# Quantised feed-forward of a gated two-layer block: the clip and the rescaling of the activations move from VectorE to ScalarE and GpSimd, in a pipeline over half tiles

## What is computed

```python
def _quantize_mx(x, ebits, mfrac, emax_elem, max_norm):        # blocks of 32 along the last axis
    amax = jnp.max(jnp.abs(xb), axis=-1, keepdims=True)
    sexp = jnp.floor(jnp.log2(jnp.where(amax == 0, 1.0, amax))) - emax_elem
    scale = jnp.exp2(jnp.clip(sexp, -127.0, 127.0))
    return _quantize_elem(xb / scale, ebits, mfrac, max_norm) * scale
def _q_act(x): return _quantize_mx(x, 2, 3.0, 2.0, 7.5)
def _mx_linear(x, w): return jnp.einsum('bsh,oh->bso', _q_act(x), _q_w(w))
gate = _mx_linear(x, w_gate)          # 512 -> 2048
up = _mx_linear(x, w_up)              # 512 -> 2048
inter = jax.nn.silu(gate) * up
return _mx_linear(inter, w_down)      # 2048 -> 512
```

## Time and profile before

| what | before |
|---|---|
| median of 3 runs | 1871.81 us |
| the profiled execution: its own time | 1870.53 us |
| its span | 1868.7 us |
| mean granted TensorE clock | 0.894 of full speed |
| busy: PE, DVE, ACT, POOL | 1484.8, 1112.7, 980.8, 635.6 us |
| stage B, from the scale of its layer norm to its last moments | 401.6 to 721.1 us |

### The profile page before, as it was taken

The page is one execution under the profiler, slowest core; times in us unless marked ns, Lnnn a source line. Parts: engine busy times, 40 slices in busy tenths (PEclk is TensorE's granted clock), DMA queues, the critical chain, the costliest instruction groups (busy, mean ns, idle before and its releaser), DMA issues. The chain is left out here.

```text
span 1868.7 us, 31243 instructions
## 1 busy us (share of the span) xinstructions
PE 1484.8 (79%) x10376; PEld 777.9 (42%) x10395; DVE 1112.7 (60%) x1785; ACT 980.8 (52%) x1503; POOL 635.6 (34%) x557
## 2 busy tenths in 40 slices
PE   6666666677776775999999711899999999999994
PEld 2444455543333332444444310444444444444442
DVE  3999999788888896888886472205415140541000
ACT  4999999733232233777777440344444444444442
POOL 3000000010000000788888535435445444544432
PEclk9778777788898897999999765999999999999998
DMA  9311100000000000000000256315335151531113
GB/s 336 135 46 46 46 1 1 29 1 1 0 0 0 0 0 1 3 2 3 2 3 3 88 190 249 117 35 163 111 86 168 26 165 34 163 95 34 30 28 102
DMA packets 49246, 118.69 MB, mean 64 GB/s; under 512 B 5536, under 2 KB 5792, under 8 KB 48576
## 3 DMA queue, kind: packets, MB, share of 16 engines
q1 hardware_dynamic: 34832, 88.53, 14.0%
q0 software_dynamic: 8176, 18.65, 5.1%
q10 hardware_dynamic: 6144, 10.28, 1.8%
HBM read 84.21 MB, written 37.43 MB: 65 GB/s over the span
## 5 line engine op out<-in xcount | busy, mean ns | idle before, releaser
L1622 PE MATMUL PS<-R 128*128 (+1 forms) x1872 | 432.7, 381 | 8.3 <-issue 7.2
L1776 DVE TENSOR_SCALAR R<-wring 128x1024 f16<-128x1024 f32 x56 | 61.5, 1108 | 382.6 <-PE PS L1645 349.2
L425 ACT ACTIVATE R<-R 128x512 bf16<-128x512 f32 x448 | 278.9, 715 | 9.4 <-PE PS L445 3.9
L1622 PEld LDWEIGHTS PS<-R 128*128 128x128 f16 x1872 | 179.5, 98 | 217.6 <-issue 19.7
L445 PE MATMUL PS<-R,ident_b 128*128 128x256 bf16 (+1 forms) x1056 | 168.6, 321 | 83.1 <-ACT R L425 79.1
L1645 PE MATMUL PS<-R 128*128 (+1 forms) x936 | 214.8, 379 | 1.2 <-ACT R L1732 1.2
L1812 POOL TENSOR_TENSOR R<-R 128x512 f32<-128x512 f32 x78 | 113.3, 1453 | 292.0 <-ACT R L1720 181.0
L871 PE MATMUL PS<-R 128*128 128x512 bf16 x495 | 141.9, 436 | 78.6 <-DVE R L807 60.4
L1036 DVE TENSOR_REDUCE R<-PS 128x1 f32<-128x512 f32 x256 | 166.6, 686 | 45.2 <-PE PS L1218 42.6
L1014 POOL TENSOR_TENSOR R<-R 128x512 f32<-128x512 f32 x128 | 166.6, 1302 | 27.8 <-ACT R L1141 12.2
L1141 ACT ACTIVATE R<-PS 128x512 f32<-128x512 f32 x256 | 144.4, 598 | 41.3 <-PE PS L1232 40.8
(11 more groups left out here) (262 smaller groups left out, 2522.3 us busy)
## 6 DMA issues: line engine op xcount, KB each, us to landing
wring<-in_L_ffn_w_kernel_dram SPq DMA_DIRECT2D x48, 512.0 KB, 5.3
slot_rows<-R SPq DMA_DIRECT2D x1, 10023.0 KB, 40.3
R<-slot_rows ACTq DMA_DIRECT2D x39, 257.0 KB, 2.7
R<-in_L_ffn_w_kernel_dram SPq DMA_DIRECT2D x16, 512.0 KB, 5.6
wring<-in_L_ffn_wo_kernel_dram SPq DMA_DIRECT2D x16, 512.0 KB, 4.5
R<-in_L_ffn_wo_kernel_dram SPq DMA_DIRECT2D x16, 512.0 KB, 4.7
X<-in_x_dram SPq DMA_DIRECT2D x4, 1024.0 KB, 9.0
R<-in_L_ffn_w_up_dram SPq DMA_DIRECT2D x4, 1024.0 KB, 10.3
```

The source lines that it names most:

```text
L425: nc.scalar.activation(marks[:, j * S:(j + 1) * S], SIM[:, tile * S:(tile + 1) * S], ACT.Sign, bias=cfloat[:, tile:tile + 1], scale=-1.0). ...
L1622: mm = nc.tensor.matmul(bank[2 * half + g], ZT[n][:, (4 * pz + k) * P:(4 * pz + k + 1) * P], weights(place, at), start=(i % 12 == 0), stop ...
```

## The change

The z quantisation and the inter quantisation are each cut in three. VectorE keeps the first part: block maxima, exponent bits, scale, reciprocal, and the rounding product, which now writes its fp8 result to a buffer of its own (bzq, biq). ScalarE copies the fp8 values to bf16 (z_widen, inter_widen). GpSimd clips them in place between CAP and -CAP and multiplies them by the scale (z_final; inter_final, in two pieces of 512). The exponent bits are taken by a tensor_tensor with a constant tile bexp and the scale by a scalar_tensor_tensor with a constant tile b16, where both were tensor_scalar.

The halves are numbered u = 0 to 31, with two buffers each of bin_, biq, bic, bib, bit2 and two PSUM banks (4 and 7) for the transposed half, and four of each scale. TensorE transposes half u-2 and multiplies half u-3 by the down weights behind gate and up of half u+1; before, both belonged to the half just made. VectorE adds tile i to X at half u = 2i+5. All loops of B are written out.

```diff
+CAP = 7.5 / 64
-        bin_ = R1[:, 11008:12032]
-        bib = R1[:, 12032:12544].bitcast(BF16)
-        bit2 = R1[:, 12544:13056].bitcast(BF16)
+        bin_ = [R1[:, 11008:12032], R1[:, 0:1024]]
+        biq = [R1[:, 1024 + 256 * n:1280 + 256 * n].bitcast(F8) for n in range(2)]
+        bic = [R1[:, 2048 + 512 * n:2560 + 512 * n].bitcast(BF16) for n in range(2)]
+        bib = [R1[:, 12032:12544].bitcast(BF16), R1[:, 3072:3584].bitcast(BF16)]
+        bit2 = [R1[:, 12544:13056].bitcast(BF16), R1[:, 3584:4096].bitcast(BF16)]
...
+            nc.gpsimd.memset(bexp, EXPONENT).then_inc(const_b, 1)
+            nc.gpsimd.memset(b16, 16.0).then_inc(const_b, 1)
...
-        def quantize_act(v, src, n, dst, base, done):
-
-
-            nb = n // BLK
-            am, pw, sc, ri = bam[:, 0:nb], bpw[:, 0:nb], bsc[:, 0:nb], bri[:, 0:nb]
...
-            nc.vector.tensor_scalar(bq[:, 0:n], bf8[:, 0:n], 7.5 / 64, -7.5 / 64, ALU.min, ALU.max).then_inc(q_step, 1)
-            v.wait_ge(q_step, base + 6)
-            nc.vector.tensor_tensor(blocks(dst), blocks(bq[:, 0:n]), spread(sc, nb), ALU.mult).then_inc(done, 1)
+        def scales(v, src, am, pw, sc, ri, n, step, base):
+            nc.vector.tensor_reduce(am, blocks(src), AX, ALU.max, apply_absolute_value=True).then_inc(step, 1)
+            v.wait_ge(step, base + 1)
+            nc.vector.tensor_tensor(pw.bitcast(I32), am.bitcast(I32), bexp[:, 0:n], ALU.bitwise_and).then_inc(step, 1)
+            v.wait_ge(step, base + 2)
+            nc.vector.scalar_tensor_tensor(out=sc, in0=pw, scalar=TINY, in1=b16[:, 0:n], op0=ALU.max,
+                                           op1=ALU.mult).then_inc(step, 1)
+            v.wait_ge(step, base + 3)
+            nc.vector.reciprocal(ri, sc).then_inc(step, 1)
+            v.wait_ge(step, base + 4)
...
+            def z_scale(j):
+                v.wait_ge(z_ready, j + 1)
+                if j > 3:
+                    v.wait_ge(zb_ready, j - 3)
+                scales(v, bz, zam, zpw, zsc[j % 4], zri, D // BLK, z_step, j * 4)
+                if j:
+                    v.wait_ge(z_wide, j)
+                nc.vector.tensor_tensor(blocks(bzq), blocks(bz), spread(zri, D // BLK), ALU.mult,
+                                        saturate=False).then_inc(z_cut, 1)
...
+            def inter_scale(u):
+                v.wait_ge(inter_ready, 2 * u + 2)
+                if u > 3:
+                    v.wait_ge(ib_ready, 2 * u - 6)
+                scales(v, bin_[u % 2], bam, bpw, bsc[u % 4], bri, 1024 // BLK, i_step, u * 4)
+                if u > 1:
+                    v.wait_ge(i_wide, u - 1)
+                nc.vector.tensor_tensor(blocks(biq[u % 2]), blocks(bin_[u % 2]), spread(bri, 1024 // BLK), ALU.mult,
+                                        saturate=False).then_inc(i_cut, 1)
...
+            z_scale(0)
+            z_scale(1)
+            for u in range(2 * NT):
+                for n in range(2):
+                    product(u, n)
+                if u % 2 and u > 4:
+                    residual((u - 5) // 2)
+                inter_scale(u)
+                if u % 2 == 0 and u // 2 + 2 < NT:
+                    z_scale(u // 2 + 2)
+                if u % 2 and u > 4:
+                    moments((u - 5) // 2)
+            residual(NT - 2)
+            moments(NT - 2)
             dve_ln_var(v, 2, 0)
-            chain(NT - 1, 1, (NT - 1) * 18 + 12)
-            finish(NT - 1)
+            residual(NT - 1)
+            moments(NT - 1)
+
+        def pool_b(pool):
+            def z_final(j):
+                pool.wait_ge(z_wide, j + 1)
+                if j:
+                    pool.wait_ge(zt_ps, j)
+                nc.gpsimd.tensor_scalar(bzc, bzc, CAP, -CAP, ALU.min, ALU.max).then_inc(z_capped, 1)
+                pool.wait_ge(z_capped, j + 1)
+                pool.wait_ge(z_cut, j + 1)
+                nc.gpsimd.tensor_tensor(blocks(bzb), blocks(bzc), spread(zsc[j % 4], D // BLK), ALU.mult).then_inc(zb_ready, 1)
+
+            def inter_final(u):
+                pool.wait_ge(i_wide, u + 1)
+                pool.wait_ge(i_cut, u + 1)
+                if u > 1:
+                    pool.wait_ge(it_ps, u - 1)
+                for n in range(2):
+                    c = slice(512 * n, 512 * n + 512)
+                    nc.gpsimd.tensor_scalar(bic[u % 2][:, c], bic[u % 2][:, c], CAP, -CAP, ALU.min, ALU.max).then_inc(i_capped, 1)
+                    pool.wait_ge(i_capped, 2 * u + n + 1)
+                    nc.gpsimd.tensor_tensor(blocks(bib[u % 2][:, c]), blocks(bic[u % 2][:, c]),
+                                            spread(bsc[u % 4][:, 16 * n:16 * n + 16], 16), ALU.mult).then_inc(ib_ready, 1)
+
+            z_final(0)
+            z_final(1)
+            for u in range(2 * NT):
+                inter_final(u)
+                if u % 2 == 0 and u // 2 + 2 < NT:
+                    z_final(u // 2 + 2)
...
+            for u in range(2 * NT + 3):
+                if u + 1 < 2 * NT:
+                    gate_up(u + 1, 0)
+                    gate_up(u + 1, 1)
+                if u % 2 == 0 and u // 2 + 1 < NT:
+                    zturn(u // 2 + 1)
+                if u == 2 * NT + 1:
+                    pe_projection(pe)
+                if 0 <= u - 2 < 2 * NT:
+                    turn(u - 2)
+                if 0 <= u - 3 < 2 * NT:
+                    down(u - 3)
...
+            def z_widen(j):
+                act.wait_ge(z_cut, j + 1)
+                if j:
+                    act.wait_ge(zb_ready, j)
+                nc.scalar.copy(bzc, bzq).then_inc(z_wide, 1)
...
+            def inter_widen(u):
+                act.wait_ge(i_cut, u + 1)
+                if u > 1:
+                    act.wait_ge(ib_ready, 2 * u - 2)
+                nc.scalar.copy(bic[u % 2], biq[u % 2]).then_inc(i_wide, 1)
...
+            for u in range(2 * NT + 2):
+                if 0 <= u - 1 < 2 * NT:
+                    inter_widen(u - 1)
+                if u == 2 * NT:
+                    act_projection(act)
+                if u + 1 < 2 * NT:
+                    silu(u + 1, 0)
+                if u % 2 and u // 2 + 2 < NT:
+                    z_widen(u // 2 + 2)
+                    if u // 2 + 3 < NT:
+                        norm(u // 2 + 3)
+                if u + 1 < 2 * NT:
+                    silu(u + 1, 1)
+                if 0 <= u - 2 < 2 * NT:
+                    icopy(u - 2)
+                if u % 2 == 0 and u // 2 + 1 < NT:
+                    zcopy(u // 2 + 1)
```

More of the change, by code:

```diff
@@ new lines, in dve_b, with product, residual @@
+        def dve_b(v):
+            def z_scale(j):
[7 more added lines that the diff above has]
+                                        saturate=False).then_inc(z_cut, 1)
+            def product(u, n):
+                v.wait_ge(silu_sb, 2 * u + n + 1)
+                v.wait_ge(gu_ps, 4 * u + 2 * n + 2)
+                nc.vector.tensor_tensor(bin_[u % 2][:, n * 512:(n + 1) * 512], bsg[:, n * 512:(n + 1) * 512],
+                                        bank[2 + n], ALU.mult).then_inc(inter_ready, 1)
+            def inter_scale(u):
[7 more added lines that the diff above has]
+                                        saturate=False).then_inc(i_cut, 1)
+            def residual(i):
+                v.wait_ge(down_ps, 2 * i + 2)
+                xt = X[:, i * D:(i + 1) * D]
@@ L837, in dve_b @@
-            for i in range(2):
-                prep(i, i * 6)
-                v.wait_ge(zb_ready, i + 1)
-            body(0, first=True)
-            with v.Fori(1, NT - 2) as i:
-                body(i)
-            body(NT - 2, last=True)
-            chain(NT - 1, 0, (NT - 1) * 18 + 6)
-            v.wait_ge(ib_ready, 2 * NT - 1)
-            finish(NT - 2)
-            dve_ln_var(v, 2, 0)
-            chain(NT - 1, 1, (NT - 1) * 18 + 12)
-            finish(NT - 1)
+            v.wait_ge(const_b, 2)
@@ L859, in zturn, with gate_up @@
                 mm.then_inc(zt_ps, 1)
[L861 to L867 removed]
+            def gate_up(u, n):
+                if u % 2 == 0 and n == 0:
+                    pe.wait_ge(zt_sb, u // 2 + 1)
+                if u:
+                    pe.wait_ge(inter_ready, 2 * u + n - 1)
                 for m in range(2):
@@ L880, in turn, with down @@
                 for c in range(8):
-                    mm = nc.tensor.transpose(bank[4].bitcast(BF16)[:, c * P:(c + 1) * P],
-                                             bib[:, c * P:(c + 1) * P], ident_b[:])
+                    mm = nc.tensor.transpose(bank[7 if u % 2 else 4].bitcast(BF16)[:, c * P:(c + 1) * P],
+                                             bib[u % 2][:, c * P:(c + 1) * P], ident_b[:])
                 mm.then_inc(it_ps, 1)
-            def down(i, half):
-                pe.wait_ge(it_sb, 2 * i + half + 1)
-                if half == 0 and beyond(i, 0):
-                    pe.wait_ge(x2_done, i)
+            def down(u):
+                pe.wait_ge(it_sb, u + 1)
+                if u % 2 == 0 and u:
```

(25 more changed lines are left out.)

175 lines of the change are left out of this document (47 added, 128 removed).

## The result

The changed kernel takes **1793.16 us** (median of 4 runs, 1790.0 to 1794.91) against 1872.28 us for the kernel before (4 runs, 1865.91 to 1873.47): ratio 0.9582, 95% interval 0.9556 to 0.9608. That is 79 us less, where the prediction had 49. The profiled execution took 1792.18 us, with a span of 1790.3.

What follows compares the result with a forecast made beforehand. VectorE's instructions were taken to bound stage B. Start 26, middle 219.5 (14 tiles of 16.0 less 4.5) and end 26 made 271.5 against 319.5 us, 48 less: 1870.5 - 48 = 1822.5, say 1823 us; range 1792 to 1856.

Steps and rivals of the forecast that it cites:

- the prediction's own case: Whole kernel: 1808 to 1836 us, around 1823, with VectorE setting stage B's pace and some port waits; chance 0.50.
- rival 1: Stage B: the shared ports cost nothing, 13.6 us per tile, 1789 us in all; chance 0.12.
- 16.0 us per tile: Middle of stage B: VectorE's own work 13.1, port waits 2.4 and 0.5 carried over from before.
- 13.1 us: VectorE in stage B: its remaining instructions per tile, gaps included, after clips and scale products leave.
- 2.4 us: Stage B: VectorE's waits per tile for ports shared with GpSimd, if blocked instructions end early; otherwise 4.0.
- the walk: One stage B tile followed, GpSimd starting 1.25 us after VectorE's rounding product, each taking free ports when asked.
- The 0.5 that before had over its own sum: VectorE's tile in stage B: 19.15 us measured against 18.6 summed, put to loop branches and cross-engine waits, kept as 0.5.
- priced at nothing by itself: VectorE's exponent and scale as two-input instructions of 16 or 32 elements: still 0.17 to 0.18 us, no added cost.
- since the rewrite: VectorE's exponent and scale: counted among instructions contending with GpSimd because they now have two SBUF inputs, six of 0.18 us.
- Rival 2: Stage B: the port exclusion costs more, 17 to 18 us per tile, 1837 to 1851 us in all; chance 0.20.
- Rival 3: Stage B: GpSimd becomes the bound and is slower than before, 20.4 us per tile, 1885 us; chance 0.10.
- Rival 4: Stage B: the pipeline gives nothing, TensorE is held and VectorE waits for gate and up, about 1868 us; chance 0.08.

Runs made afterwards that it cites:

- e2: The changed kernel with GpSimd's clips and scale products in stage B replaced by memsets of the same size: 1774.37 us, 12.27 us per tile.
- e6: The changed kernel with ScalarE casting the even half ahead of its two copies, so GpSimd starts earlier: 1796.21 us.
- e7: The changed kernel with GpSimd's clip and product of an inter half each as one instruction of 1024 instead of two of 512: 1800.31 us.
- e4: The changed kernel with every GpSimd clip in stage B done twice: 1810.65 us.
- e3: The changed kernel's order, buffers and depth, but clip and scale product back on VectorE, no cast, GpSimd idle: 1861.62 us, 0.9937 of the kernel before.
- e1: The changed kernel with exponent and scale taken by one-input tensor_scalar instructions again, as before the change: 1791.37 us.
- e9: The changed kernel without pipeline depth, TensorE transposing the half just made, work still on ScalarE and GpSimd: 1998.49 us, 1.0678 of the kernel before.

## Why the prediction was right, and where it was off

The direction and the mechanism held: VectorE stays the pace (96% busy), TensorE fits under it, GpSimd and ScalarE don't bind, and the stages around B don't move. The size was 30 us short: 1793 lies 15 us under the 1808 to 1836 of the prediction's own case and 1 us inside the stated range, which reached so low only for the upper half of rival 1, so that the range holds it is in part luck. The middle was to take 219.5 us and took 189.2, 30.4 less. Start and end, predicted at 26 each, took 24.1 and 23.6, and the 4.3 us that they were better cancel by chance against the 4.3 that the rest of the program was longer.

The middle rests on the term "16.0 us per tile" (measured: 13.51 on average, 13.61 steady). Its three parts:

- **"13.1 us" of VectorE's own work was 12.2** (e2). The durations were right: 1.22, 0.35 and 1.22 for what stands alone, and 0.19 for exponent and scale, for which the 0.18 of the earlier trace rows belongs to the one-input form. The gaps were not. The prediction put 0.04 us between all neighbours, but that holds only where one waits for the other. Independent ones overlap: the rounding product from 501.08 for 1.57 ends at 502.65, and z's maxima start at 502.57; the two products and the addition likewise (504.59 + 1.28, next at 505.78).
- **"2.4 us" for the ports was 1.38** in the steady tile, 1.24 by e2. The rule was right, the walk's phases were not. It let GpSimd begin 1.25 us after each rounding product. For the even half it was 2.24 (502.65 to 504.89), because the cast (503.75 to 504.81) stood behind ScalarE's copies of the transposed half and of z (502.36 and 503.27), and so z's rounding product met nothing. GpSimd was also faster than priced, 0.61 and 1.05 unblocked instead of 0.76 and 1.16, with 0.09 between them instead of 0.15, and the odd rounding product met an opening. e6 shows that the phase alone is worth some 0.4 us per steady tile, and e7 and e4 that longer GpSimd instructions cost what the exclusion says.
- **"The 0.5 that before had over its own sum"** did not come back. The trace of the kernel before has it where a tile's loop turns: ahead of the tile's first product VectorE stands idle behind its own last instruction, 14 times and 7.9 us, 0.56 per tile. For TensorE it waits 2.5 us at the products in the whole stage, and 2.8 at the additions. e3 and the change, with the loops written out, have no such pause. Waits of the kernel before, 430 to 698 us:

```profile
DVE R L807 <- DVE R L789: 7.9, 14, 0.6
```

Together 0.9 + 1.0 + 0.5 = 2.4 us per tile, 33.5 us in 14 tiles. Against them stands that the prediction took 4.5 us off for what tiles 1 and 14 lack, where the middle is only 1.4 shorter than 14 steady tiles, its uneven first tiles included: 33.5 - 3.1 = 30.4.

The other steps: exponent and scale "priced at nothing by itself" is right (e1). But it is not "since the rewrite" that they meet GpSimd, as the one-input form waits as well. The cast of 1.05 took 1.052. TensorE's wait "below 40" is 27.1, the clock "above 0.88" is 0.98. The written-out loops cost nothing, as said, and with them the pause above is gone.

The rivals. Rival 1, that the ports cost nothing, gave 1789 us, nearer the result than my own case, and is nevertheless refuted: e2 shows 19 us of port waits. Its number came close because its base of 13.6 per tile was too high by as much as the ports cost: 0.9 of own work and 0.5 of loops, against 1.4. Rival 2 (17 to 18 per tile) did not occur: blocked instructions end early, 1.08 after the release, and in the steady tile only three meet anything. Rival 3 needed a pair of 2.8 us and the pair is 1.66; neither the repeated operand nor 16 bits cost anything. Rival 4 did not occur here, but e3 and e9 show how near it lies: the pipeline without the shift to the other engines is worth only 0.6% [0.4%, 0.8%], and the shift without the pipeline loses 6.8% [6.5%, 7.1%]. With the pipeline there, the shift brings the other 68 us.

## What to carry to other kernels

Work may go from a saturated VectorE to GpSimd even though GpSimd is slower at it, if the consumer runs far enough behind that GpSimd's latency is hidden; make that depth first, since without it the same shift turned 4% of gain into 7% of loss. Price the shared ports by laying both engines' instructions side by side in time, with the start of GpSimd's work taken from everything queued on the engine that feeds it, and keep GpSimd's pieces short. When VectorE is the pace, sum starts to starts, not durations and gaps.
